# Routed down weights kept on the core for the last three steps of a gated two-layer block

## The reference, cut to what matters

```python
x = x + tanh(g_xattn[0]) * L0_xattn(layernorm(x), ctx, ...)   # tanh over rows x 77 text rows: "the scan"
x = x + tanh(g_ffn[0])   * L0_ffn(layernorm(x), ...)
x = x + tanh(g_xattn[1]) * L1_xattn(layernorm(x), ctx, ctx, ...)
x = x + tanh(g_ffn[1])   * L1_ffn(layernorm(x), ...)
# L1_ffn: topk_idx, tw = route(x)                     16 experts, 4 per row
#   h, u = x @ gate_w[e], x @ up_w[e];  y = (silu(h) * u) @ down_w[e]
#   routed = sum over the 4 chosen e of tw * y;  shared = silu(x @ sg) * (x @ su) @ sd
```

## Time and profile before

| | us |
|---|---|
| median of 3 runs | 1557.78 |
| lowest and highest | 1555.26, 1567.31 |
| the profiled execution, its own time | 1560.64 |
| span of its profile | 1558.8 |

### The profile page before, as it was taken

The page is one execution under the profiler, slowest core; times in us unless marked ns, Lnnn a source line. Parts: engine busy times, 40 slices in busy tenths (PEclk is TensorE's granted clock), DMA queues, the critical chain, the costliest instruction groups (busy, mean ns, idle before and its releaser), DMA issues.

```text
span 1558.8 us, 36097 instructions
## 1 busy us (share of the span) xinstructions
PE 1318.7 (85%) x12356; PEld 790.5 (51%) x12356; DVE 964.7 (62%) x2339; ACT 1093.5 (70%) x1805; POOL 530.3 (34%) x505
## 2 busy tenths in 40 slices
PE   5777687787588999998999899989997887998991
PEld 2212242333234554755475546554666576777771
DVE  7987647635853675378537874896469875324442
ACT  5998886777696899879987997769872442333330
POOL 1101121122263221425543545256427634024223
PEclk8978987989798999999999999999998998999996
DMA  7654502403132366355434554535346746689994
GB/s 225 221 195 115 128 1 68 135 7 87 49 107 50 108 177 156 83 152 164 151 89 136 161 149 115 147 93 161 101 126 195 198 135 172 172 223 284 243 248 123
DMA packets 251594, 220.28 MB, mean 141 GB/s; under 512 B 130906, under 2 KB 206242, under 8 KB 251426
## 3 DMA queue, kind: packets, MB, share of 16 engines
q1 hardware_dynamic: 224993, 170.78, 41.3%
q0 software_dynamic: 12288, 33.57, 7.0%
q10 hardware_dynamic: 14144, 13.63, 2.6%
HBM read 114.20 MB, written 76.45 MB: 122 GB/s over the span
## 4 chain that ended last, share of the span: by engine, by line
PE 49%; DVE 20%; ACT 20%; issue 6%; POOL 3%; DMA 1%; POOLq 0%; SPq 0%; DVEq 0%; ACTq 0%
ACT tanh_tiles L1280 16%; PE psF L1048 8%; PE psE L893 6%; PE psE L895 5%; PE psE L894 5%; PE psY L893 3%; PE psY L895 3%; PE psY L894 3%; PE psF L893 2%; PE psF L899 2%; PE psF L895 2%; PE psF L894 2%; POOL work L879 2%; PE psF L1219 1%; DVE xc L1630 1%
## 5 line engine op out<-in xcount | busy, mean ns | idle before, releaser
L1280 ACT ACTIVATE tanh_tiles<-feat,text_bias 128x512 f32<-128x512 f32 x1232 | 774.4, 714 | 65.8 <-DVE feat L1671 57.1
L1048 PE MATMUL psF<-tanh_tiles,wslide 128*32 128x512 f32 x2464 | 364.3, 652 | 58.5 <-ACT tanh_tiles L1280 57.9
L1700 DVE TENSOR_TENSOR tile<-tile,psE 128x512 f32<-128x512 f32 x136 | 92.9, 683 | 161.4 <-PE psE L895 101.9
L1299 ACT CAST hid<-tile 128x512 f16<-128x512 f32 x136 | 83.5, 614 | 145.2 <-DVE tile L1700 143.3
L893 PE MATMUL psY<-down,hid 128*128 128x256 f16 x544 | 150.5, 277 | 23.4 <-issue 16.5
L824 POOL TENSOR_TENSOR hid<-tile,hid 128x512 f16<-128x512 f32 x76 | 88.4, 1164 | 229.1 <-ACT hid L1299 228.6
L893 PE MATMUL psE<-xg,up_hi 128*128 128x128 f16 x832 | 160.1, 219 | 1.5 <-ACT tile L1307 1.2
L850 POOL DMA_INDIRECT xs_rows<-xs,slot_i x128 | 126.7, 990 | 98.6 <-issue 36.1
L894 PE MATMUL psE<-xg,up_hi 128*128 128x128 f16 x832 | 160.1, 219 | 0.0
L895 PE MATMUL psE<-xg,up_lo 128*128 128x128 f16 x832 | 159.8, 219 | 0.0
L893 PE MATMUL psE<-xg,gate_hi 128*128 128x128 f16 x832 | 153.5, 220 | 7.1 <-issue 6.2
(11 more groups left out here) (311 smaller groups left out, 2895.1 us busy)
## 6 DMA issues: line engine op xcount, KB each, us to landing
down<-down_split SPq DMA_DIRECT2D x224, 256.0 KB, 3.4
xs_rows<-peakT SPq DMA_DIRECT2D x32, 512.0 KB, 5.9
y_rows<-hid SPq DMA_DIRECT2D x52, 256.0 KB, 2.6
y_rows<-tanh_tiles ACTq DMA_DIRECT2D x52, 256.0 KB, 3.0
down_split<-hid SPq DMA_DIRECT2D x18, 256.0 KB, 3.1
xscan<-in_x SPq DMA_DIRECT2D x8, 512.0 KB, 5.8
x<-in_x SPq DMA_DIRECT2D x8, 512.0 KB, 5.3
w_lin<-w_split SPq DMA_DIRECT2D x15, 256.0 KB, 3.1
```

The source lines that it names most:

```text
L1048: last = pe.matmul(psF[32 * j:32 * j + 32, RHO, :], wslide[:, c, 31 - g:63 - g], tanh_tiles[:, st.at(SETS, 2 * g + c) % HRING, j], start=g ...
L1280: act.activation(tanh_tiles[:, n % HRING, j], feat[:, c], ACT.Tanh, bias=text_bias[:, c, col:col + 1]).then_inc(h_ready, 1)
L1299: act.copy(hid_hi[:, n], tile[:, v.n % 2]).then_inc(ghi_done, 1)
L1700: dve.tensor_tensor(tile[:, n], tile[:, n], psE[:, (2 * v.n + 1) % 3], ALU.mult).then_inc(g_done, 1)
```

## The change

The scan's memory (`tanh_tiles`, `xscan`, `feat`) becomes one tensor `arena` of 32 KB a partition, which has room for the down weights of all 16 routed experts. In the ninth step SP loads them there, one expert of 256 KB every third slot, and from the tenth step on the down matmuls of routed units read them at addresses in registers. A second block of register instructions, `down_addresses`, stands one slot before each such unit's first `down_part`. The per-block loads end with the ninth step; the last shared expert's two loads go to `w_lin` and `w_scan`. `LATE` moves to s = 9. The copies of late units go to `down`. The gathers' ring becomes two buffers for group 1 (`w_kv`, `texts`) and four for the later groups (`work` and `xn`).

```diff
+IN_WORK = 16
+RESIDENT = 5
-LATE = STEPS * SLOTS
+LATE = (STEPS + 1) * SLOTS
@@ plan: late set ahead; entries (loads into down) only for units before LATE
+        v.late = v.routed and v.at >= LATE
+        if v.at < LATE:
...
+        arena = sb("arena", [P, E * 2 * KC * D // 2])
...
+        resident = arena[:, :].bitcast(F16).rearrange("p (e h k d) -> p e h k d", e=E, h=2, k=KC)
...
+        rows_ring = [w_kv[:, :, :, :]..., texts[:, 0:NT * D]...]
+        rows_ring += [work[:, 1024 * n:1024 * (n + 1)]... for n in range(3)] + [xn[:, :, :]]
+        y_late = [down[:, n].rearrange("p a b c -> p (a b c)").bitcast(F32) for n in range(4)]
+        down_last = [w_lin, w_scan]
...
         def buffer(n):
-            return (n - IN_XSCAN) % ROWS_RING
+            return n % 2 if n < IN_WORK else 2 + n % (len(rows_ring) - 2)
@@ SP, slot
+                if v and not v.routed and v.f and v.at >= LATE:
+                    sp.wait_ge(wo_ps, 2 * STEPS)
+                    sp.dma_start(down_last[v.e - E]..., down_dram[v.e]).then_inc(last_loaded, 16)
+                if s == STEPS and i >= RESIDENT and (i - RESIDENT) % 3 == 0 and (i - RESIDENT) // 3 < E:
+                    e = (i - RESIDENT) // 3
+                    if e == 0:
+                        sp.wait_ge(rho_part, STEPS * SETS)
+                    sp.dma_start(resident[:, e]..., down_dram[e]).then_inc(resident_loaded, 16)
@@ GpSimd, gather
-                if n >= IN_XSCAN + ROWS_RING:
-                    pool.wait_ge(added, n - ROWS_RING + 1)
+                if g and user_before(n) is not None:
+                    pool.wait_ge(added, user_before(n) + 1)
+                if n == IN_WORK:
+                    pool.wait_ge(placed, GROUPS)
@@ TensorE
+            def down_addresses(v):
+
+                word = pe.value_load(ids[0:1, v.g % 3, v.pair:v.pair + 1])
+                down_owners[v.n] = [pe.snap((word >> (4 * b)) & 15, min_val=0, max_val=E - 1) for b in range(2)]
+                for e in down_owners[v.n]:
+                    for c in range(2 * KC):
+                        pe.lower_val((e * (2 * KC * D) + c * D) * 2)
@@ down_part
-                n = v.entries[b if v.routed else 0]
-                pe.wait_ge(down_loaded[n % 4], 16 * (n // 4 + 1))
+                if v.late:
+                    pe.wait_ge(resident_loaded, 16 * E)
+                    e = down_owners[v.n][b]
+                    w = [[resident[:, bass.ds(e, 1), h, f]... for f in range(2)] for h in range(2)]
...
                     last = product(psY[...], [(hid_hi[:, v.n % 4, cut[f]], hid_lo[:, v.n % 4, cut[f]],
-                                               down[:, n % 4, 0, f], down[:, n % 4, 1, f])
+                                               w[0][f], w[1][f]) for f in range(2)])
@@ TensorE, slot
+                v = began(T, DOWN - 1)
+                if v and v.late:
+                    down_addresses(v)
```

More of the change, by code:

```diff
@@ L177, in plan @@
         v.n = n
[L178 to L181, removed]
+        v.late = v.routed and v.at >= LATE
+        if v.at < LATE:
+            if v.routed:
+                v.entries = (entries, entries + 1)
+            elif v.f:
+                v.entries = (entries,)
         entries += len(v.entries)
         v.bank = len(freed)
-        v.late = v.routed and v.at >= LATE
         if v.routed or v.f:
@@ L301, in build @@
         w_dram = nc.dram_tensor("w_split", [4, P, 2 * KC * D], F16, kind="Internal").ap()
-        Wkh, Wkl, Wvh, Wvl = (sb(n, [P, KC, D], F16) for n in ("Wkh", "Wkl", "Wvh", "Wvl"))
+        w_kv = sb("w_kv", [P, 4, KC, D], F16)
+        Wkh, Wkl, Wvh, Wvl = (w_kv[:, n] for n in range(4))
         w_lin, w_scan = sb("w_lin", [P, 2, KC, D], F16), sb("w_scan", [P, 2, KC, D], F16)
@@ L313, in build @@
         lower = sb("lower", [P, E, E], F16)
-        text_bias = sb("text_bias", [P, KC, B * TXT])
+        texts = sb("texts", [P, 2 * KC * B * TXT])
+        words = KC * B * TXT
+        text_bias = texts[:, 0:words].rearrange("p (k t) -> p k t", k=KC)
+        ctxT_hi, ctxT_lo = (texts[:, words + n * words // 2:words + (n + 1) * words // 2].bitcast(F16).rearrange("p (k t) -> p k t", k=KC)
+                            for n in range(2))
         scan_norm = sb("scan_norm", [P, 2, 2, NT])
@@ L1008, in down_part @@
                         pe.wait_ge(y_used, count)
-                n = v.entries[b if v.routed else 0]
-                pe.wait_ge(down_loaded[n % 4], 16 * (n // 4 + 1))
+                if v.late:
+                    pe.wait_ge(resident_loaded, 16 * E)
+                    e = down_owners[v.n][b]
+                    w = [[resident[:, bass.ds(e, 1), h, f].rearrange("p o d -> p (o d)") for f in range(2)] for h in range(2)]
+                elif v.entries:
+                    n = v.entries[b if v.routed else 0]
+                    pe.wait_ge(down_loaded[n % 4], 16 * (n // 4 + 1))
+                    w = [[down[:, n % 4, h, f] for f in range(2)] for h in range(2)]
+                else:
+                    pe.wait_ge(last_loaded, 32)
+                    w = [[down_last[v.e - E][:, h, f] for f in range(2)] for h in range(2)]
                 if v.routed:
@@ L1020, in down_part @@
                                        [(hid_hi[:, (v.n - 1 + f) % 4, cut], hid_lo[:, (v.n - 1 + f) % 4, cut],
-                                         down[:, n % 4, 0, f], down[:, n % 4, 1, f]) for f in range(2)])
+                                         w[0][f], w[1][f]) for f in range(2)])
                 last.then_inc(y_ps, 1)
+                if b:
+                    down_owners.pop(v.n, None)
             def positions(g):
@@ L1610, in place @@
                 dve.tensor_copy(slot_i[:, g % 3, mine], slot_f[:, mine]).then_inc(slots_ready, 1)
[L1611 removed]
+                dve.tensor_reduce(wk[:, g % 3, mine].rearrange("p c k -> p k c"), pick_w[:, :, mine], AX, ALU.add).then_inc(placed, 1)
+                dve.wait_ge(placed, g + 1)
             def add_shared(v, b):
```

31 lines of the change are left out of this document (17 added, 14 removed).

## The result

The changed kernel takes 1635.18 us (median of 4 runs, 1632.4 to 1639.25), the kernel before 1558.93 us in the same pairs (4 runs): ratio 1.048, interval [1.0435, 1.0532]. It is slower by 76 us. The profiled execution took 1639.25 us, its span is 1637.5.

The account below looks back on a forecast made before the run. It took TensorE's sequencer, full with register work, as the tail's bound. Terms 71.0 + 3 - 2.1 - 2 = +69.9 gave 1630.5 us for the profiled execution, 1628 us for the median; range 1602 to 1652.

Parts of the forecast that it names:

- The bound: Expert tail: TensorE's sequencer is full and sets 5.43 us a unit, so any added register instruction is paid in full.
- Loads come two a unit: Sign of being right: in the tail TensorE's register loads would come two a unit, units 7.2 to 7.5 us apart.
- The unit's growth: Late routed unit in the tail: second block +1.17, register addresses +0.85, existing load -0.10, together 1.92 us, to 7.35.
- Rival 1: Down matmuls: high weight's address worked out twice, 12 register instructions instead of 8; +17, 1645 us; chance 0.08.
- The count: Tenth step on: 37 units at 1.92 us (+71.0), +3 beside the shared expert's units, -2.1 at the end.
- The ninth step: Changed roles of VectorE, ScalarE and GpSimd: -2 us, bounds -8 to +6; over 135 us would show the prediction wrong.
- The end: Very end of the tail: two waits for down loads go, -2.1 us.
- The existing load: First block's register load in the tail gets relief from fewer transfers: -0.10 us a unit, between -0.19 and 0.
- The clock: Sign of being wrong: a granted clock under 0.9 in the tail.
- rival 2: Tail: the clock falls, at 1.2 GHz the array needs 8.0 us a unit; at most +24, 1652 us; chance 0.02.
- Rivals 3 and 5: 3: tail register work half hidden, 1580 us, chance 0.05. 5: resident weights late, first late down part waits; small, inside range.
- Rival 4: Tail: transfers set the pace, the sequencer has room and taking off loads gives -7.6; 1546 us; chance 0.05.

Follow-up runs that it names:

- e5_late: Kernel before with only `LATE` moved to the tenth step, so ninth-step low halves go to GpSimd and copies to VectorE; 1563.25 us, ratio 1.003.
- e3_lows: Changed kernel with only the ninth step's low halves put back on VectorE; 1626.67 us, ratio 1.0441.
- part 3: Ninth-step runs: changed kernel with low halves back on VectorE (ratio 1.0441); kernel before with both roles, gather ring or copies changed (1.003, 0.9999, 1.0006).
- e1_fixed: Changed kernel with late down matmuls reading resident weights at fixed addresses, without second register block or their routing choice; 1565.31 us, ratio 1.0044.
- part 4: Kernel before with less register work: two units' expert numbers packed into one word (1552.66 us), then also no precomputed address sums (1551.87 us).
- w1_packed: Kernel before with two units' expert numbers packed into one word, so TensorE and SP load every second unit only; 1552.66 us, ratio 0.996.
- x1_copy: Changed kernel with VectorE copying resident weights into the `down` buffers, fixed addresses for TensorE's down matmuls and the old ninth-step roles; 1618.19 us, ratio 0.9955.
- the last version: x1_copy plus packed expert words and no precomputed address sums; 1609.18 us, ratio 0.9911 to the kernel before, and 0.9902 when run again.
- e2_cached: Changed kernel with down addresses worked out once, for the first late unit, and its registers reused by all later units; 1567.75 us, ratio 1.0067.
- e4_noload: Changed kernel with expert numbers kept from the first block's registers: no second load or unpacking, address instructions stay; 1605.46 us, ratio 1.0295.
- w2_packed_lean: w1_packed with the register block's precomputed address sums left out too; 1551.87 us, ratio 0.9961 to the kernel before.
- e7_copies: Kernel before with only the ninth step's copies out of PSUM moved from ScalarE to VectorE; 1626.02 us against 1626.12, ratio 1.0006.

## Why the prediction was right, and where it wasn't

I forecast 1628 us with a range of 1602 to 1652; 1635 came out. The mechanism in the tail was the one forecast; that the total lies as near as 7 us is in part luck, since two errors of opposite sign stand in it.

- **The bound.** Right. The waits, the group of `arena` matmuls and the step from 5.38 to 6.49 to 7.26 us a unit, with register instructions as the only difference, show the sequencer. Loads come two a unit. By the Trainium skill, Advanced Engine Details and Errata, section Sequencer Loop, other engine instructions can be read and queued while the sequencer's own code executes. Here they weren't: the new register work came as +1.83 us a unit and a hole of 1.10 us. I had written that the rule fails for instructions behind a load whose result they need. That is too narrow. The matmul behind the hole of 0.50 us reads `down` at a fixed address, and the one behind the hole of 0.72 us uses addresses that the other block had made; neither needs the word being loaded, and both came after the whole block.
- **The unit's growth**, 1.92 us (1.6 to 2.6): right, 7.26 - 5.43 = 1.83. My split (1.17 for the block, 0.85 for the eight addresses, -0.10 for the old load) wasn't tested term by term: the runs give 1.11 us for the block's sums with the eight address instructions and 0.77 for load and unpacking. Rival 1 (the high address twice, 12 instructions) fell: between 1400 and 1500 us, 13.8 units, the new register instructions at L921 are 54, four a unit, one for each low weight, and L920 has 278, 20 a unit: 16 for gate and up as before and four for the high weights.
- **The count**, 37 x 1.92 + 3 - 2.1 = +71.9 from the tenth step on: measured +57.3 + 6.0 + 0.8 = +64. The term was too large by 8 us. The second blocks say where (the first row is the whole kernel, the second from 1359 to 1596 us):

```profile
L1010 PEldq TENSOR_LOAD <-ids x40: 297/302/575, 1320.6 to 1604.9; - x40
...
L1010 PEldq TENSOR_LOAD <-ids x31: 297/302/537, 1375.6 to 1593.3; - x31
```

31 of the 40 blocks stand among the 33 units that grew by 57.3 us, and 31 x 1.83 = 57: these were forecast well. The other nine, six between 1320.6 and 1350.3 us and three at the very end, grew the time by 6.0 and 0.8 us in place of the forecast's 12.4.
- **The ninth step**, forecast -2 (bounds -8 to +6): measured +11.6. This is the step of the prediction that failed, in sign and beyond its bounds. The step had weighed the engines' busy sums, with 71 of 123 us on GpSimd. What decided was when GpSimd got to a low half: it stands behind four gathers that start 1.3 to 2.0 us apart, and silu and product wait through it. `e5_late` shows +8.1 for both roles with nothing else changed, and `e3_lows` gets 5.2 us back by the low halves alone; how much of the rest is the copies' is open (part 3). The step was to keep its 123 us within 8 and took 134.7 (1168.3 to 1303.0 us, against 1165.3 to 1288.3), a hair under the 135 that I had named as a sign of being wrong. The count's error of -8 us and this one of +14, with 3 us ahead of the ninth step, leave the sum for the profiled execution 9 us short: 69.9 against 78.7.
- **The end**, -2.1: measured +0.8. The wait for down loads is gone, but the last three units' register blocks stand at the same place: from 1596 us on the array waits 2.5 us for "issue" before down matmuls, a little more than it had waited for the loads.
- **The existing load**, -0.10 for fewer transfers (bounds -0.19 and 0): it fell to the far bound, from 488 to 301 ns, and not for the reason given. `e1_fixed` has fewer transfers too, DMA share 0.61, and its load takes 464.
- **The clock.** 0.96 in the tail, above the 0.9 that I had named as a sign of being wrong, so rival 2's condition wasn't met. Rivals 3 and 5: 1.83 us were paid of 1.92 priced, so next to no register work was hidden, and no wait for the resident weights stands in the tail.
- **Rival 4** was wrong for this kernel, since taking off the loads (`e1_fixed`) brought nothing by itself that stands clear of the scatter: 5.39 us a unit against 5.43. But part 4 shows transfers as the next bound, close behind.

What stays open: the split of the ninth step's 11.6 us beyond the low halves (part 3), where the 0.4% of `w1_packed` lies, where `x1_copy` gains in the ninth step, the 3.0 us ahead of the ninth step (the kernel before and the eight runs made where it takes 1557 to 1559 us have that mark between 1158.8 and 1165.3 us, so 3.0 is less than their scatter), and the gain of the last version under those conditions.

## What to carry to other kernels

An engine that is 90% busy may be bound by what feeds it. Count its register instructions in a unit of work and price them by the pitch of a stretch in which the queue has run dry, before adding one more run-time address. Put the address work on an engine that has room, and let it hand over data at a fixed place. Here that, with the old roles in the ninth step, turned +5% into -0.45%, and with less register work on top into -1%. When work moves to a half-empty engine, ask what stands ahead of it in that engine's order at that moment, not whether the busy sums have room.

## What the runs showed of the hardware

- **A register address costs in its making, not in its use.** 5.38 us a unit with matmuls at addresses kept in registers (`e2_cached`), 5.39 with fixed ones (`e1_fixed`).
- **A load into a register costs more than it lasts.** One of 0.30 us with three instructions of unpacking is 0.77 us of a unit (6.49 in `e4_noload`, 7.26 in the changed kernel).
- **TensorE's register work holds up matmuls that don't need it.** In the kernel before a down matmul with a fixed weight address came 1.27 us after the start of the next unit's block, behind a hole of 0.50 us; in the changed kernel the like is a hole of 0.72 us.
- **The load's length isn't set by traffic.** 464 and 458 ns at a DMA share of 0.61 to 0.64, 301 at 0.43 to 0.51, but 308 in `w2_packed_lean` at a share of 1.02. What sets it isn't settled: the first thought, that it waits behind matmuls already queued, fits the changed kernel and `e1_fixed`, and doesn't fit `w2_packed_lean`, whose array is as full (162.08 of 172 us) as that of `e1_fixed` (163.47 of 178).
- **The kernel before itself** took 1557 us (median of 18 runs) on one occasion and 1626 (of 23) on another, 4.4% apart. Only ratios of pairs made together can be compared across them. The profile of `e7_copies`, which is as fast as the kernel before by its ratio, shows where its 66 us lie: 15 ahead of the ninth step, 25 between its marks, 13 from there to the tail and 13 in the tail's 33 units. The granted clock from 1180 to 1390 us was 0.84, where the kernel before has 0.96 and 0.90 in the like stretches. Why it was lower isn't known.
